# A wait behind every fourth gather on GpSimd in a routed mixture-of-experts layer

## The reference, cut to what matters

```python
idx, w = _route(xf, Wr, br)                       # 6 of 32 experts a row
gate = jnp.zeros((T, E), w.dtype).at[jnp.arange(T)[:, None], idx].add(w)
def step(acc, ew):
    w1, w2, g = ew
    h = jnp.square(jax.nn.relu(xf @ w1.T)) @ w2.T # 256 -> 128 -> 256
    return (acc + g[:, None] * h, None)
acc, _ = jax.lax.scan(step, jnp.zeros_like(xf), (W1, W2, gate.T))
shared = jnp.square(jax.nn.relu(hidden_tensor @ Ws1.T)) @ Ws2.T
...
x = x + s * g                                     # g = silu(shared + acc)
```

## Time and profile before

| what | us |
|---|---|
| median of 3 executions | 406.76 |
| lowest and highest | 404.17 and 406.96 |
| the profiled execution, its own time | 402.68 |
| its span | 400.9 |

### The profile page before, as it was taken

How to read it: one execution, slowest core, us unless ns; L and a number is a source line. 1 busy time by engine, 2 the same in 40 slices (tenths; PEclk the granted TensorE clock), 3 DMA queues, 4 the chain that set the end, 5 groups by cost and what they waited for, 6 DMA issues and landing times.

```text
span 400.9 us, 8217 instructions
## 1 busy us (share of the span) xinstructions
PE 312.5 (78%) x2716; PEld 235.8 (59%) x2716; DVE 274.6 (69%) x647; ACT 239.5 (60%) x382; POOL 222.2 (55%) x235
## 2 busy tenths in 40 slices
PE   0576986999978888697988888899947967978750
PEld 0344743677767676575756757675713755866630
DVE  4688889989932756475766645756505857998686
ACT  5788799545765766675866757966504525434341
POOL 2966879848756364546636454104774665556600
PEclk9997799899989989999899999999976999999986
DMA  8941150444842464547446463525634564666721
GB/s 273 367 160 54 61 183 13 152 156 165 287 127 94 154 192 127 173 138 233 155 126 195 135 206 108 182 86 195 181 108 112 154 195 144 183 176 199 188 72 66
DMA packets 40490, 62.90 MB, mean 157 GB/s; under 512 B 5218, under 2 KB 28930, under 8 KB 40450
## 3 DMA queue, kind: packets, MB, share of 16 engines
q1 hardware_dynamic: 33202, 42.57, 33.1%
q0 software_dynamic: 7248, 19.80, 16.7%
HBM read 46.66 MB, written 15.70 MB: 156 GB/s over the span
## 4 chain that ended last, share of the span: by engine, by line
PE 44%; DVE 20%; issue 12%; DVEq 8%; ACT 6%; another core or an unknown queue 5%; POOL 2%; DMA 2%; SPq 1%; ACTq 0%
PE rot L908 5%; DVE xs L1281 5%; PE hp L931 4%; DVEq L1283 4%; PE hp L933 3%; PE hp L946 3%; PE hp L944 2%; PE hp L945 2%; PE bp L891 2%; PE hp L932 2%; DVE hf L1257 2%; PE rot L961 2%; PE rot L959 2%; PE dp L1002 2%
## 5 line engine op out<-in xcount | busy, mean ns | idle before, releaser
L605 POOL DMA_INDIRECT xgt<-xtab,ids x91 | 92.4, 1015 | 69.2 <-PE rot L908 43.3
L687 ACT ACTIVATE hf<-hf 128x512 f32<-128x512 f32 (+2 forms) x80 | 49.9, 624 | 86.8 <-DVE hf L1257 52.6
L616 POOL DMA_INDIRECT wst<-ytab,slot x60 | 61.6, 1027 | 38.8 <-DVE xs L1281 25.0
L1000 PE MATMUL dp<-wt,hhi 128*128 128x256 f16 x204 | 57.4, 281 | 7.9 <-DVE hlo L1264 4.3
L1003 PE MATMUL dp<-wt,hhi 128*128 128x256 f16 x204 | 57.3, 281 | 4.0 <-issue 4.0
L1274 DVE COPY wst<-rot 128x512 f32<-128x512 f32 (+1 forms) x35 | 23.8, 681 | 51.5 <-PE rot L961 43.5
L1002 PE MATMUL dp<-wt,hlo 128*128 128x256 f16 x204 | 57.4, 281 | 0.5 <-issue 0.3
L944 PE MATMUL hp<-xh,wt 128*128 128x512 f16 (+1 forms) x148 | 51.1, 345 | 7.6 <-issue 4.7
L1257 DVE SCALAR_TENSOR_TENSOR hf<-hp,gate_bc 128x512 f32<-128x512 f32 x48 | 32.9, 685 | 33.7 <-remote 19.3
L692 ACT ACTIVATE hhi<-hf 128x512 f16<-128x512 f32 (+2 forms) x80 | 49.9, 624 | 5.7
L946 PE MATMUL hp<-xh,wt 128*128 128x512 f16 (+1 forms) x148 | 51.4, 347 | 0.7 <-issue 0.7
(11 more groups left out here) (174 smaller groups left out, 718.5 us busy)
## 6 DMA issues: line engine op xcount, KB each, us to landing
gate_bc<-gtab SPq DMA_DIRECT2D x48, 256.0 KB
ytab<-wst SPq DMA_DIRECT2D x45, 256.0 KB
wst<-in_wts SPq DMA_DIRECT2D x17, 512.0 KB, 5.7
xs<-in_x SPq DMA_DIRECT2D x4, 512.0 KB, 4.6
xn<-in_x SPq DMA_DIRECT2D x16, 128.0 KB
out<-xn SPq DMA_DIRECT2D x16, 128.0 KB
xtab<-xn SPq DMA_DIRECT2D x3, 512.0 KB, 3.1
xgt<-xtab,ids POOLq DMA_INDIRECT x91
```

Of the source, the lines that this page charges most:

```text
L605: nc.gpsimd.indirect_dma_start(xg[:, a % XRING, :, :].rearrange("p h d -> p (h d)"), None, xtab, bass.IndirectOffsetOnAxis(ids[:, a:a + 1] ...
L616: nc.gpsimd.indirect_dma_start(yk[:, n % KRING, :], None, ytab, bass.IndirectOffsetOnAxis(slot[:, n // K, n % K:n % K + 1], 0))\
L687: nc.scalar.activation(hf[:, k % HP, 0:width(k)], hf[:, k % HP, 0:width(k)], ACT.Square, scale=W_SCALE ** (-0.5 if gated else -1.0))
L1000: nc.tensor.matmul(o, hhi[:, k % HRING, hcols], hi, start=(e == 0 and q % 2 == 0), stop=False, skip_group_check=True)
```

## The change

Ahead of gather a, where a is a multiple of four and not zero, GpSimd now waits for the landing of each of the four gathers before it. The same holds for the gathers of results. For the gathers of x's rows that is at a = 4, 8, ... 88 (22 places), for those of results at n = 4, 8, ... 56 (14 places), each with four waits.

```diff
             for a in range(TILES):
                 if a >= XRING:
                     pool.wait_ge(t_done, a - XRING + 1)
+                if a >= J and a % J == 0:
+
+                    for b in range(a - J, a):
+                        pool.wait_ge(xg_landed[b % XRING], 16 * (b // XRING + 1))
                 nc.gpsimd.indirect_dma_start(xg[:, a % XRING, :, :].rearrange("p h d -> p (h d)"), None, xtab,
                                              bass.IndirectOffsetOnAxis(ids[:, a:a + 1], 0))\
                   .then_inc(xg_landed[a % XRING], 16)
@@
             def gather_result(n):
                 if n >= KRING:
                     pool.wait_ge(yk_used, n - KRING + 1)
+                if n >= J and n % J == 0:
+
+                    for b in range(n - J, n):
+                        pool.wait_ge(yk_landed[b % KRING], 16 * (b // KRING + 1))
                 nc.gpsimd.indirect_dma_start(yk[:, n % KRING, :], None, ytab,
                                              bass.IndirectOffsetOnAxis(slot[:, n // K, n % K:n % K + 1], 0))\
                   .then_inc(yk_landed[n % KRING], 16)
```

## The result

The changed kernel takes 427.69 us (median of 4 runs, 426.26 to 430.77), the kernel before beside it 405.64 us (4 runs, 404.17 to 406.96). The ratio is 1.056, with a 95% interval of 1.048 to 1.063. I had forecast 401.4 us, in a range of 390 to 415. The kernel is slower by what rival C describes, and by more than C allowed. The profiled execution took 428.56 us with a span of 426.8, which is 25.9 us more span than before. Where the executions of a kernel fall into a faster and a slower group, its ratio is taken from the faster ones alone, here and in all that follows.

The account below looks back on a forecast made before the run. TensorE and VectorE, 64% of the chain, were taken as the bound, with stalls beside long gather runs. Results -6.4 us and x's rows +1.0 made -5.4 us: 406.76 to 401.4 us, range 390 to 415.

Parts of the forecast that it names:

- rival C: Both gather streams: waiting for landings becomes the bound, slower, up to +12.5 us (419.3 us) at L = 2.6; chance 0.27.
- L: One landing added to the four issues of each gather batch on GpSimd; taken as 2.0 us, range 1.4 to 2.6.
- My lower bound of 1.4: Least landing time, read from the result gather of 327.64, whose issue ends at 328.59 and traffic at 330.00.
- My upper bound of 2.6: Most landing time, from the gather of 281.56: issue ended at 282.51, the addition needing it began without idle time.
- Gathers of x's rows: Slot groups: 20 batches of 7.26 us against the present 7.17, mostly covered; +1.0 us, out of 0 to 9.9.
- the cover: Ring of eight for x's rows: last gather ends 6.5 us before its tile is turned, 4.5 spare after the landing.
- Gathers of results: Result collection: 15 batches of 7.16 us, no lasting cover, gathers end at 387.4, span 394.5 instead of 400.9; -6.4 us.
- The sum: Whole kernel: -6.4 for results plus 1.0 for x's rows, -5.4 us, put on the median 406.76, giving 401.4 us.
- the stalls: Result collection: three VectorE relu waits, 19.3 us together, longest 11.3, coinciding with long unbroken gather runs; expected to go.
- Rival A: Result collection: the stalls are not the gathers' doing and stay; only +1.0 us, 407.8 us, no change; chance 0.15.
- "remote": Wait-list entry under which VectorE's relu waited three times while results are collected, 19.3 us in total.
- the signs for C: Slot groups: TensorE waiting at L908 for xgt, and the last gather of x's rows well behind 256.

Follow-up runs that it names:

- older four: Changed kernel, but every fourth gather waits for the four before the last four, so up to eight are in flight: 402.97 us, ratio 1.000 to the kernel before.
- ring-of-eight kernel: Kernel before with the ring of result buffers cut from 12 to 8, no landing waits: 397.72 us with the stall, 364.65 us on the chip without.

## Why the prediction was wrong

**The step that failed: the stop costs L + 0.30 with L = 2.0 us, so 2.3 us.** It costs 3.27 us in the mean, nearly 1 us more, 36 times. It failed in both of its terms. The landing behind the end of the issue is 2.50 us in the mean and 1.70 at least. My lower bound of 1.4 was taken from the end of the traffic, and the signal of a landing comes later than the last packet: by 0.31 to 0.53 us in 35 of the 36 stops and by 1.08 in one. My upper bound of 2.6, meant to hold for the mean, came from one gather at the head of a run; it does hold, but the middle of the two was half a microsecond short. The other term, the 0.30 us, was the gap between two gathers that wait for nothing. Behind a landing it is 0.77 us, for which I had no row. In the prediction's terms, the effective L was 3.27 - 0.30 = 2.97, beyond the 2.6 at which I ended the range. With the landing alone at 2.5 its formulas give +8.9 us; the 0.47 us beside it make up the other 17.

The Trainium skill, "DMA: Bandwidth & Descriptors", section "Anatomy of one DMA — SWDGE (gpsimd) path", gives about 2.0 us and the bytes over 436 GB/s, an estimate of 2.3 us for such a gather. Setup is part of that figure, so it counts from the start of the issue, while L begins at its end; the prediction put the one in the other's place. The trace has 2.6 us at least from the start of the issue and 3.2 to 3.5 in the median of the fourth gathers. The measurement decides.

**Gathers of x's rows: +1.0 forecast, +17.4 measured.** The formula held. With 2.97 it gives 20 x (5.26 + 2.97 - 7.17) - 3.5 = 17.7 us, the 3.5 being what is left of the cover of 6.5. The stops it is worked out from hold no wait for TensorE's turning, as the constant 0.77 us shows, so this is more than the pace put in another way; the run with x's waits alone, at +20.4, agrees. I had written that every 0.1 us of L costs 2 us once the cover is gone. It was gone: the deficit of 1.06 us a batch uses 3.5 us up in four batches. TensorE's granted clock may have a share in it: it is 0.93 of full speed (2.4 GHz) in the stretch of x's rows (the stretches above), where the kernel before has 0.97 from 95 to 250. Its idle pieces are more, so this may be a consequence; how much of the 17.4 us it is can't be taken apart here.

**Gathers of results: -6.4 forecast, +8.5 measured.** Here 15 batches of 8.13 in place of 7.16 us are 14.6 us more, and -6.4 + 14.6 = 8.2. Nothing else is needed. Waits among results alone measured +5.3 and +7.9 us on two chips.

**The sum.** With L = 2.97 in both places the prediction's own formulas give 280.29 + 17.7 + 15 x 8.13 - 0.3 + 7.1 = 426.7 us of span; the span is 426.8. The 2.97 is taken from this same run, so that is a check of the formulas and not a second forecast.

**What was right.** That the stalls go when the gathers are broken into fours: with a stop at every fourth result they went, in the two kernels without one (x's waits alone, older four) they were back at 9 to 12 us. Rival A fell by this, but only for chips that have the stall. Two readings beside it were off. "They begin only after 8 or more gathers in a row, all three times" holds for the third alone: the first begins at 289.10, during the seventh gather, the second at 302.63, during the first gather behind a pause, the third at 325.77, during the eighth of its run. And "remote" was no sign against TensorE, whose own signal it was. That the gather stream is what is late next: the chain's 34%. C's mechanism was right; the size at which I placed its upper end was the error.

**The signs I had named.** GpSimd idle 1.5 to 2.5 us before every fourth gather: wrong, 2.46 is the least. No relu idle over 3 us under "remote": right. 15 or more matmuls in each 2 us: right, 15 to 19 in each of the ten stretches from 298. VectorE waiting at L1281 for landings: right. Last gather of results near 385: wrong, 417.88. Of the signs for C, both came: TensorE waits for xgt, 18.3 us, and the last gather of x's rows ends at 275.

## What to carry to other kernels

When an issuing engine is made to wait for its own transfers, price the stop as landing from the end of the issue plus the time until the next issue, with the mean landing and not the best one (here 2.50 + 0.77 us; the least was 1.70), multiply by the number of stops, and compare the batch with the pace that its users need; a batch that lands exactly on the present pace has no margin, and then every tenth of a microsecond counts as often as there are batches. If long runs of transfers hurt, try what costs no round trip (a smaller ring), or stop less often, at eight instead of four; here each gained 1.3 to 2.0% on the chips with the stall. Read a wait's end from the semaphore that it waits for where the list's name decides an argument: here "remote" was TensorE and "TensorE" was a landing. And before a stall is engineered away, see on a second chip whether it is there.

## What the runs showed of the hardware that I had not expected

**Two kinds of chip.** The same kernel before takes 402.5 to 405.6 us in the first comparison and on three chips of the experiments, and 363.78 us on another. The ring-of-eight kernel was profiled on both kinds, 397.29 and 365.44 us, and stretches of equal length show where they part. On a chip with the stall:

```profile
0.00:90.00 90.00, 63.17 (x476) 43.03 (x477) 73.13 (x256) 65.93 (x111) 63.39 (x80) 0.92 0.47 157
91.00:250.00 159.00, 138.33 (x1381) 110.53 (x1380) 100.13 (x192) 106.15 (x154) 91.43 (x90) 0.96 0.55 164
```

and on the one without:

```profile
0.00:90.00 90.00, 61.66 (x471) 41.59 (x472) 72.94 (x256) 65.21 (x110) 62.60 (x80) 0.91 0.47 157
91.00:250.00 159.00, 148.52 (x1575) 122.77 (x1573) 115.26 (x222) 122.66 (x182) 96.90 (x93) 1.00 0.60 183
```

Up to 90 us, before the first gather (91.8 and 92.3 us), they are alike: 476 and 471 matmuls. In the next 159 us, which are the gathers of x's rows, the one gets 1381 matmuls done and the other 1575, with a clock of 0.96 and 1.00. So on the slower kind TensorE loses something over the whole stretch in which the gathers run, not only in the stalls that I had read; that the gathers are the cause there is likely, not shown. x's last gather begins at 251.4 there and at 229.2 here. The gathers are no quicker to land on this chip than the fourth gathers of the changed kernel above; the view of L616, still the ring of eight, says

```profile
L616 POOL DMA_INDIRECT wst<-ytab,slot x60: 942/946/1406, 257.7 to 350.4; - x60
...
DMA to landing us min/median/max: 2.7/3.6/6.2
```

It is what runs beside them that isn't held up: VectorE waited for one landing in that run, 1.8 us. The two kinds also part in what the traces have of semaphores. Of the 4976 signals that the transfers of this kernel send when they land, the trace of the slower chip has 2657, that of the faster 4938. Up to 90 us it is 577 and 576, so records go missing from about the first gather on. Whether that has the same cause as TensorE's stalls, or the recording itself holds TensorE up, nothing here tells, as no execution without recording is there to compare.

Why TensorE is held up on one kind of chip and not on the other stays open. That runs of gathers set the stall off is shown on the slower kind alone.

**GpSimd's own operations between gathers.** Six small subtractions of 0.4 us with drains, put between gathers, made a pause of 6.3 us in the mean, with up to 7.92 us before the second of them. I had expected 2.4. No run here tells what GpSimd is doing in that time.
